# Two layers of attention over eight images: when the squares for the bound run, where the selected rows' products stand, how the weighted sums are grouped in image 1, and how many filler matmuls stand in the tail

## The chip, the cores and the metric

The kernel runs on one core of one Trainium2 chip. The metric is the device time in microseconds of one execution, and the number of a kernel is the median of its runs. The core has five engines that run side by side: TensorE (PE in the rows, with its weight loads as PEld), VectorE (DVE), ScalarE (ACT), GpSimd (POOL) and SyncE (SP, which here only issues DMAs). Each works through its own list of instructions in order and waits on semaphores for the others.

## What is computed

Eight images of 32 x 32 positions and 128 channels go through two blocks. The first is a normalisation, full attention with 8 heads of 16 channels over all 1024 positions, a projection and a residual. The second projects, normalises, and lets each position attend to 16 of 64 pooled keys, the 16 with the largest score over all heads and positions:

```python
# layer 0, for each image
qkv = layernorm(x) @ w_qkv + b_qkv
attn = softmax(q @ k.T * HEAD_DIM ** -0.5)          # 8 heads, 1024 x 1024
x = x + (attn @ v) @ w_out + b_out
# layer 1
tokens = x @ Win + b_in
t = layernorm(tokens); q, k, v = t @ Wq, t @ Wk, t @ Wv
pk, pv = pool4x4(k), pool4x4(v)                      # 64 pooled positions
red = (q @ pk.T).max(over heads and positions)       # 64 numbers
idx = top_k(red, 16)
tokens = tokens + softmax(q @ pk[idx].T * scaling) @ pv[idx]
tokens = tokens + gelu(layernorm(tokens) @ Wf1 + bf1) @ Wf2 + bf2
out = tokens @ Wout + bout
```

## The kernel before

**The steps.** Layer 0's attention of an image is cut into 32 steps (`STEPS`): four pairs of heads, each with eight blocks of 128 keys. In a step TensorE computes the scores of one key block for two heads and all queries in two halves c = 0 and 1 (`scores`, L616, into the two halves of the PSUM tile `S`), ScalarE takes the exponential of each half (L850, `Pr<-S`), and TensorE multiplies with the values (`weighted`, L631, into `O`). Each half of `S` has one buffer, so the scores of step s, half c, wait for the exponential of step s-1, half c (`probs_ready`). `Pr` holds three steps.

**Grouping of the weighted sums.** In images 0 and 7 the weighted sum of step s-1 follows the scores of step s. In the others two sums, of s-2 and s-1, follow the scores of each even step. After each eighth step VectorE turns the finished `O` of the head pair (`divide_o`, L1067 to L1074: transpose, reciprocal, product, transpose); the first weighted sum of the next pair waits for the first of these (`o_turned`).

**The work between.** Other work is hung on the steps by hand. `before_tasks(n + 1, s)` prepares the next image: transposes of xn, q and k (steps 17 to 23), v, the squares' sums for a bound (`AT_BOUND` = 28) and a flag (30); with steps above 32 it runs in the image itself (the `tokx` products at 32 and 37, steps 0 and 5 of the image). `after_tasks(n - 1, s)` does layer 1 of the image before, by a table of steps (`USUAL`, and `ENDING` for the last two images): `tok` at step 3, `t` 12, `q1` 13, `pk` 15, scores against pooled keys 18 to 21, `rt` 22 and `rb` 23. At `rb` VectorE ranks the 64 maxima (L1154 to L1163) and writes `hot`, the one-hot rows of the ranks (`hot_ready`). At `sel` TensorE multiplies `hot` with the pooled keys and values (L696, L698), VectorE writes `bd_k` and `bd_v` from it, and at `s2` (step 27) TensorE multiplies by `bd_k` (L645).

**GpSimd.** Within an image it moves `tokx`, computes `means_share` and `q1_rest`, normalises the image after the next, and then in `square(n)` (L488) squares `qh` and `kh` of the next image, once VectorE has drained k at step 23. The sums of these squares are a bound on the scores; TensorE uses them at step 28. Behind it stand the copies of the next image's values (`place_v`).

**The tail.** Image 7's layer 1 and the end of image 6's come after all attention (`tail()`). There TensorE has little work between waits, and ahead of certain steps it runs filler matmuls whose result is not used (L834, two for each count in `WARM`).

In the trace a matmul on f32 operands appears as two instructions, so a weighted sum of one step is 8 rows of L631 in it and 4 in the order of the program; the scores (f32r) appear as 4 in both.

Of the kernel before, what the change touches and what calls it, by code (L numbers as in the profile page):

```python
# [31 lines left out]
IMAGES, SIDE, C = 8, 32, 128  # L32
# [8 lines left out]
STEPS = PAIRS * TILES  # L41
# [13 lines left out]
AT_XN, AT_XN_SECOND = (6, 10), (8, 10)  # L55
AT_Q, AT_K, AT_V, AT_TOKX = (17, 19), (21, 23), (25, 29), (32, 37)
AT_BOUND, AT_FLAG = 28, 30
After = namedtuple("After", "tok norm1 t q1 pk sc rt rb sel s2 exp2 e2 pt tok2 norm2 tt2 t2 ff gelu wout out")
USUAL = After(tok=3, norm1=8, t=12, q1=13, pk=15, sc=(18, 19, 20, 21), rt=22, rb=23, sel=26, s2=27, exp2=28, e2=28, pt=30,
              tok2=31, norm2=34, tt2=33, t2=37, ff=(39, 39), gelu=39, wout=40, out=(41, 43))  # L60
ENDING = After(tok=3, norm1=8, t=12, q1=13, pk=14, sc=(17, 18, 19, 20), rt=21, rb=22, sel=23, s2=24, exp2=25, e2=25, pt=27,
               tok2=28, norm2=30, tt2=29, t2=32, ff=(33, 33), gelu=33, wout=34, out=(35, 36))
# [3 lines left out]
def tail():  # L66

    last = [(IMAGES - 1, s) for s in range(AFTER_END)]
    before = [(IMAGES - 2, s) for s in range(STEPS, AFTER_END)]
    k, m = ENDING.wout - STEPS, ENDING.tok + 1  # L70
    return before[:k] + last[:m] + before[k:] + last[m:]


def plan(n):

    return ENDING if n >= IMAGES - 2 else USUAL


def one_by_one(n):

    return n in (0, IMAGES - 1)


def xn_steps(n):
# [1 line left out]
    return AT_XN_SECOND if n == 1 else AT_XN  # L86


WARM = {ENDING.tok: 4, ENDING.t: 28, ENDING.pk: 8, ENDING.sc[0]: 36, ENDING.sel: 8, ENDING.pt: 16, ENDING.t2: 22, ENDING.out[0]: 8}
WAKE = 24  # L90

K_TOK, K_T, K_Q1, K_PK, K_PV, K_SC, K_RT, K_RB, K_SELK, K_SELV = 0, 2, 4, 6, 7, 8, 16, 17, 18, 19
# [38 lines left out]
def two_layers(nc, x, ln_scale, ln_bias, w_qkv, b_qkv, w_out, b_out, Win, b_in, Wq, Wk, Wv, g1, be1, g2, be2,  # L131
# [11 lines left out]
    with ExitStack() as ctx:  # L143
        def sb(name, shape, dt=fp32):
            return ctx.enter_context(nc.sbuf_tensor(name, shape, dt))

        def sem(name):
            return ctx.enter_context(nc.semaphore(name))
# [37 lines left out]
        tok, tT, q1T = sb("tok", [P, TILES, C]), sb("tT", [P, T]), sb("q1T", [P, T])  # L186
# [59 lines left out]
        pooled_ready, hot_ready = sem("pooled_ready"), sem("hot_ready")  # L246
# [12 lines left out]
        def a_after(n, use, i):  # L259

            return a_turn_of[n, use, i] + 1
# [14 lines left out]
        def wait_for_flag(eng, n):  # L276

            if n == 0:
                eng.wait_ge(first_dve, FIRST_FLAG)
            else:  # L280
                eng.wait_ge(a_drained, a_after(n, "flag", 0))
# [142 lines left out]
        def _(pool):  # L424
            def wait(signal, value):

                pool.wait_ge(signal, value)
                pool.sem_inc(pool_passed, 1)
# [55 lines left out]
            def square(n):  # L484

                wait(a_drained, a_after(n, "k", 1))
                for i, part in enumerate((qh, kh)):
                    ins = pool.tensor_tensor(squares[:, i, :], part[:, :].bitcast(fp32), part[:, :].bitcast(fp32), ALU.mult)  # L488
                ins.then_inc(squares_ready, 1)
# [12 lines left out]
            def image(n):  # L502

                if n > 0:
                    place_v(n, 3)
                    wait(b_drained[1], b_after(n - 1, K_TOK + 1))
                    wait(a_drained, a_after(n, "tokx", 1))
                else:
                    wait(first_dve, FIRST_DVE)
                pool.tensor_tensor(tokx[:, :, :], tokx_new[:, :, :], tok_bias[:, :].unsqueeze(1).to_broadcast([P, TILES, C]),  # L510
                                   ALU.add).then_inc(tokx_moved, 1)
                if n == 0:
                    normalise(1)
                if n + 1 < IMAGES:
                    means_share(n + 1)
                if n > 0:
                    q1_rest(n - 1)
                if n == 0:
                    square(1)
                if n + 2 < IMAGES:  # L520
                    normalise(n + 2)
                if 0 < n < IMAGES - 1:
                    square(n + 1)
                if n + 1 < IMAGES:
                    for j in range(3):
                        place_v(n + 1, j)
# [7 lines left out]
        def _(pe):  # L534
# [49 lines left out]
            def row_maxima(n):  # L584

                for j in range(PAIRS):
                    pe.wait_ge(stack_in[j], 32 + 16 * STACK_DMAS * (n + 1))
                if n > 0:
                    pe.wait_ge(probs_ready, 2 * STEPS * n)
                pe.sem_inc(pe_passed, 1)  # L590
                with pe.Fori(0, TILES) as t:
                    pe.wait_ge(tile_copied, TILES * n + t + 1)
                    for h in range(HEADS):
                        pe.wait_ge(max_drained, MAX_TILES * n + HEADS * t + h + 1)
                        r = 64 * (h % 2)
                        for c in range(2):
                            mm = pe.matmul(S[:, h % 2, c * HALF:(c + 1) * HALF], Qt[r:r + MROW, h // 2, :],
                                           Ks[r:r + MROW, h // 2, c * HALF:(c + 1) * HALF], start=True, stop=True)
                        mm.then_inc(max_filled, 1)
                pe.wait_ge(max_drained, 2 + MAX_TILES * (n + 1))  # L600
                pe.sem_inc(pe_passed, 1)
                pe.transpose(S[0:MAX_TILES, 0, 0:P], mx[:, :], ident[:, :]).then_inc(max_turned, 1)
                pe.wait_ge(mneg_ready, n + 1)
                pe.wait_ge(mrow_in, 16 * HEADS * (n + 1))

            def scores(n, s, c):

                j, kb = s // TILES, s % TILES
                before = 2 * STEPS * n + 2 * s + c - 1
                if before > 0:  # L610
                    pe.wait_ge(probs_ready, before)
                if kb == 0 and c == 0:
                    pe.wait_ge(stack_in[j], 32 + 16 * STACK_DMAS * (n + 1))
                for a in range(2):
                    head = slice(64 * a, 64 * a + MROW + 1)
                    mm = pe.matmul(S[:, c, a * HALF:(a + 1) * HALF], Ks[head, j, kb * P:(kb + 1) * P],  # L616
                                   Qs[head, j, c * HALF:(c + 1) * HALF], start=True, stop=True)
                mm.then_inc(scores_ready, 1)

            def weighted(n, s):  # L620

                j, kb = s // TILES, s % TILES
                pe.wait_ge(probs_ready, 2 * STEPS * n + 2 * s + 2)
                if kb == 0:
                    pe.wait_ge(va_ready, PAIRS * n + j + 1)
                    if n > 0 or j > 0:
                        pe.wait_ge(o_turned, PAIRS * n + j)
                for a in range(2):
                    for c in range(2):
                        r = 32 * (2 * a + c)  # L630
                        mm = pe.matmul(O[r:r + 32, :], Va[:, kb, 2 * j + a, :], Pr[:, (STEPS * n + s) % 3, c, a * HALF:(a + 1) * HALF],  # L631
                                       start=(kb == 0), stop=(kb == TILES - 1))
                mm.then_inc(pv_done, 1)
# [161 lines left out]
            def image(n):  # L795

                wait_for_flag(pe, n)
                pe.sem_inc(pe_passed, 1)
                with pe.If(pe.value_load(flag[0:1, 0:1], min_val=0, max_val=HEADS) > 0):
                    row_maxima(n)  # L800
                with pe.Else():
                    pe.sem_inc(max_filled, MAX_TILES)
                    pe.sem_inc(max_turned, 1)
                for s in range(STEPS):
                    scores(n, s, 0)
                    scores(n, s, 1)
                    if s > 0 and (s % 2 == 0 or one_by_one(n)):
                        if not one_by_one(n):
                            weighted(n, s - 2)
                        weighted(n, s - 1)  # L810
                    if n > 0:
                        before_tasks(n, STEPS + s)
                    if n + 1 < IMAGES:
                        before_tasks(n + 1, s)
                    if n > 1:
                        after_tasks(n - 2, STEPS + s)
                    if n > 0:
                        after_tasks(n - 1, s)
                if not one_by_one(n):
                    weighted(n, STEPS - 2)  # L820
                weighted(n, STEPS - 1)

            image(0)

# [4 lines left out]
            for n, s in tail():  # L829
                for _ in range(WARM.get(s, 0) if n == IMAGES - 1 else 0):  # L830

# [496 lines left out]
```

## Time and profile before

| | us |
|---|---|
| median of 3 runs | 860.02 |
| the 3 runs | 860.02, 855.59, 860.54 |
| profiled execution, its own time | 855.3 |
| its span, first to last instruction | 853.6 |
| PE, ACT, DVE, POOL busy in the span | 796.4, 603.8, 519.4, 163.7 |
| mean granted TensorE clock | 0.972 |

All times of rows are microseconds from the start of the span. A row of the timeline gives start, duration, engine, line, operation and tiles; in square brackets stands how long the engine was idle just before and what ended the wait. The granted clock is a share of full speed: 1.00 is 2.4 GHz, 0.50 is 1.2 GHz.

### The profile page before, as it was taken

To read this page: it belongs to the slowest core of one execution; us is meant where nothing else is said; L and a number is where in the kernel's file an instruction comes from. 1 tells how busy PE (TensorE), PEld (TensorE's weight loads), DVE (VectorE), ACT (ScalarE), POOL (GpSimd) and SP (SyncE) were. 2 spreads that over 40 slices of the span, in tenths; PEclk is the share of its full clock that TensorE was granted. 3 is DMA by queue.
4 is the path that set the end of the run, shared out by engine and by line. 5 is a ranking of instruction groups with operands and counts; after the bars stand their busy time and mean duration, and the time that the engine had idled before them with its cause. 6 is when DMAs were issued, how large, how long until landed. Compare 5 with 4: busy or idle time off the path is not lost.

```text
span 853.6 us, 14509 instructions
## 1 busy us (share of the span) xinstructions
PE 796.4 (93%) x5155; PEld 382.9 (45%) x5155; DVE 519.4 (61%) x1518; ACT 603.8 (71%) x683; POOL 163.7 (19%) x198
## 2 busy tenths in 40 slices
PE   8889888999999999999999999999999989899988
PEld 6322332345443545345434544344533534246675
DVE  6405434678567775678567765767467853467464
ACT  3697775777887788777886788768876787682112
POOL 1620520410341031220241033202111011000100
PEclk9999987999999999999999999999999999899979
DMA  3553341422442251432342352323152232201300
GB/s 67 96 90 65 64 81 31 100 47 49 82 98 46 48 87 45 104 63 48 66 109 45 52 97 66 75 48 63 26 122 47 43 66 50 56 7 31 76 1 25
DMA packets 45309, 52.91 MB, mean 62 GB/s; under 512 B 15920, under 2 KB 33968, under 8 KB 45232
## 3 DMA queue, kind: packets, MB, share of 16 engines
q1 hardware_dynamic: 45232, 51.92, 31.3%
q8 instruction: 43, 0.70, 0.3%
q14 instruction: 34, 0.28, 0.1%
HBM read 5.45 MB, written 4.19 MB: 11 GB/s over the span
## 4 chain that ended last, share of the span: by engine, by line
PE 61%; ACT 13%; DVE 8%; issue 5%; ACTq 0%; DVEq 0%
PE O L631 21%; PE S L616 13%; ACT Pr L850 9%; PE BC L645 6%; PE BC L637 3%; PE S L834 3%; PE BC L742 2%; PE BC L682 2%; PE BC L728 2%; PE A L569 2%; PE BC L664 2%; DVE rsel L1159 1%; DVE rgt L1158 1%; ACT hT L890 1%; ACT L850 1%
## 5 line engine op out<-in xcount | busy, mean ns | idle before, releaser
L850 ACT ACTIVATE Pr<-S 128x1024 f32<-128x1024 f32 x512 | 491.0, 1029 | 136.3 <-PE S L616 132.8
L631 PE MATMUL O<-Pr,Va 128*32 128x512 f32 x2048 | 263.7, 623 | 8.5 <-DVE OT L1067 7.8
L616 PE MATMUL S<-Qs,Ks 49*128 49x512 f32 x1024 | 217.5, 470 | 30.2 <-ACT Pr L850 27.4
L616 PEld LDWEIGHTS S<-Qs,Ks 49*128 49x128 f32 x1024 | 87.8, 185 | 173.2 <-ACT Pr L850 132.4
L631 PEld LDWEIGHTS O<-Pr,Va 128*32 128x32 f32 x2048 | 51.9, 111 | 117.1 <-issue 96.3
L496 POOL TENSOR_TENSOR q1l<-q1T,q1h 128x1024 fp32r<-128x1024 f32 x8 | 19.1, 2389 | 226.5 <-DVE q1h L1117 226.5
L1141 DVE TENSOR_REDUCE r<-BC 128x1 f32<-128x512 f32 x64 | 41.3, 684 | 29.8 <-PE BC L682 29.4
L1067 DVE STREAM_TRANSPOSE OT<-O 128x512 f32<-128x512 f32 x32 | 22.8, 713 | 55.1 <-PE O L631 54.9
L459 POOL TENSOR_SCALAR xn<-X,ln 128x128 f32<-128x128 f32 x56 | 45.8, 830 | 3.9 <-DVE ln L980 3.9
L865 ACT ACTIVATE tT<-BC,cols 128x512 f32<-128x512 f32 x32 | 23.4, 779 | 31.5 <-PE BC L637 31.4
L510 POOL TENSOR_TENSOR tokx<-tokx_new,tok_bias 128x1024 f32<-128x1024 f32 x8 | 18.9, 2366 | 121.0 <-DVE tokx_new L986 121.0
L488 POOL TENSOR_TENSOR squares<-qh 128x1024 bf16<-128x1024 f32 x7 | 13.6, 1937 | 140.5 <-DVE kl L994 140.5
L1208 DVE TENSOR_SCALAR hT<-BC,cols 128x512 f32<-128x512 f32 x32 | 24.0, 751 | 25.0 <-PE BC L728 23.5
L470 POOL COPY Va<-v_new 128x256 f32<-128x256 f32 x32 | 11.9, 399 | 139.8 <-PE O L631 120.8
L1213 DVE TENSOR_TENSOR Y<-BC,out_bias 128x512 f32<-128x512 f32 x16 | 11.0, 690 | 45.1 <-PE BC L742 45.1
L481 POOL TENSOR_SCALAR tokx_new<-win_sum,ln 128x128 f32<-128x128 f32 x64 | 37.4, 607 | 1.4 <-POOL tokx L510 1.3
L834 PE MATMUL S<-Qs,Ks 49*128 49x512 f32 x260 | 33.6, 410 | 0.0
L728 PE MATMUL BC<-tT,wf_s 128*128 128x512 f32 x64 | 31.7, 616 | 1.1 <-ACT tT L865 0.5
L682 PE MATMUL BC<-Q1s,K1s 96*128 96x512 f32 x64 | 29.7, 539 | 3.2 <-issue 2.2
L742 PE MATMUL BC<-w2o,hT 128*128 128x128 f32 x256 | 32.2, 280 | 0.0
L742 PEld LDWEIGHTS BC<-w2o,hT 128*128 128x128 f32 x256 | 29.6, 192 | 5.1 <-issue 5.1
L569 PE MATMUL A<-xnT,wqkv_s 128*128 128x512 f32 x56 | 31.5, 645 | 0.0
(189 smaller groups left out, 995.6 us busy)
## 6 DMA issues: line engine op xcount, KB each, us to landing
Qs<-qh SPq DMA_DIRECT2D x128, 64.0 KB, 2.3
Ks<-kh SPq DMA_DIRECT2D x128, 64.0 KB, 2.3
Q1s<-q1h SPq DMA_DIRECT2D x64, 128.0 KB, 2.4
X<-in_x_dram SPq DMA_DIRECT2D x8, 512.0 KB, 4.0
Qs<-ql SPq DMA_DIRECT2D x64, 64.0 KB, 2.4
Ks<-kl SPq DMA_DIRECT2D x64, 64.0 KB, 2.3
attnT<-On SPq DMA_DIRECT2D x128, 32.0 KB, 2.0
Q1s<-q1l SPq DMA_DIRECT2D x32, 128.0 KB, 2.4
```

Source lines behind the costliest of these rows:

```text
L459: ins = pool.tensor_scalar(xn[:, t, :], X[:, t, :], ln[:, 0, t:t + 1], ln[:, 1, t:t + 1], ALU.subtract, ALU.mult)
L481: ins = pool.tensor_scalar(tokx_new[:, t, :], win_sum[:, :], ln0[n % 2][:, 0, t:t + 1], None, ALU.mult)
L569: pe.matmul(A[:, :], wqkv_s[:, c:c + C], half(xnT, h), start=True, stop=True).then_inc(a_filled, 1)
L616: mm = pe.matmul(S[:, c, a * HALF:(a + 1) * HALF], Ks[head, j, kb * P:(kb + 1) * P], Qs[head, j, c * HALF:(c + 1) * HALF], start=True, sto ...
L631: mm = pe.matmul(O[r:r + 32, :], Va[:, kb, 2 * j + a, :], Pr[:, (STEPS * n + s) % 3, c, a * HALF:(a + 1) * HALF], start=(kb == 0), stop=(k ...
L645: mm = pe.matmul(bank[:, t * P:(t + 1) * P], lhs[:, c:c + P], w, start=(i == 0), stop=(i == len(pairs) - 1))
L682: pe.matmul(bank[:, :], K1s[:, j, :, :].rearrange("p a b -> p (a b)"), half(Q1s[0:ROWS1, j, :], h), start=True, stop=True).then_inc(filled, 1)
L728: pe.matmul(bank[:, :], wf1_s[:, f * C:(f + 1) * C], half(tT, h), start=True, stop=True)\
L742: mm = pe.matmul(BC[h][:, t * P:(t + 1) * P], hT[:, f, c:c + P], w2o[:, f, :], start=False, stop=(t == 3 and f == 1))
L834: pe.matmul(S[:, 0, a * HALF:(a + 1) * HALF], Ks[head, 0, 0:P], Qs[head, 0, 0:HALF], start=True, stop=True)
L850: act.activation(Pr[:, g % 3, c, :], S[:, c, :], ACT.Exp, scale=SCALE).then_inc(probs_ready, 1)
L1141: ins = dve.tensor_reduce(r8[:, 2 * j + h:2 * j + h + 1], bank[:, :], AX.X, ALU.max)
```

## The change

There are four edits. `square(n)` for n > 1 also waits for `hot_ready` of the image whose ranks are computed in the same stretch. `sel` in `USUAL` moves from step 26 to 25 (images 0 to 5, whose layer 1 runs inside images 1 to 6). In image 1 the weighted sums of steps 0 to 11 are issued one by one, each behind the scores of the next step; from step 14 on they go in pairs as before. And `WARM` is smaller at four places of the tail (`t` 28 to 8, `sel` 8 to 4, `pt` 16 to 12, `t2` 22 to 20) and has no entry any more for `out[0]` (8 before).

```diff
+LIGHT = 13
-USUAL = After(... rt=22, rb=23, sel=26, s2=27, exp2=28, ...
+USUAL = After(... rt=22, rb=23, sel=25, s2=27, exp2=28, ...
...
-def one_by_one(n):
-
-    return n in (0, IMAGES - 1)
+def sums_behind(n, s):
+
+    if n in (0, IMAGES - 1) or (n == 1 and s < LIGHT):
+        return (s - 1,) if s > 0 else ()
+    return (s - 2, s - 1) if s % 2 == 0 and s > 0 else ()
...
-WARM = {ENDING.tok: 4, ENDING.t: 28, ENDING.pk: 8, ENDING.sc[0]: 36, ENDING.sel: 8, ENDING.pt: 16, ENDING.t2: 22, ENDING.out[0]: 8}
+WARM = {ENDING.tok: 4, ENDING.t: 8, ENDING.pk: 8, ENDING.sc[0]: 36, ENDING.sel: 4, ENDING.pt: 12, ENDING.t2: 20}
...
             def square(n):
 
                 wait(a_drained, a_after(n, "k", 1))
+                if n > 1:
+                    wait(hot_ready, n - 1)
...
-                    if s > 0 and (s % 2 == 0 or one_by_one(n)):
-                        if not one_by_one(n):
-                            weighted(n, s - 2)
-                        weighted(n, s - 1)
+                    for behind in sums_behind(n, s):
+                        weighted(n, behind)
...
-                if not one_by_one(n):
-                    weighted(n, STEPS - 2)
-                weighted(n, STEPS - 1)
+                for behind in sums_behind(n, STEPS):
+                    weighted(n, behind)
```

How the change stands in the order of instructions, at three places. On TensorE at the start of image 1, from step 0 to the transposes of xn behind step 6 (`S` scores, `O` weighted sums, `A` the tokx products and the transposes of xn, `BC` the product for tok), before:

```order
143 L616 MATMUL S<-Qs,Ks 128x512 x4
144 L645 MATMUL A<-win_s,xhT 128x128 x4
145 L616 MATMUL S<-Qs,Ks 128x512 x8
146 L631 MATMUL O<-Pr,Va 32x512 x8
147 L616 MATMUL S<-Qs,Ks 128x512 x4
148 L645 MATMUL BC<-wow,attnT 128x128 x8
149 L616 MATMUL S<-Qs,Ks 128x512 x4
150 L631 MATMUL O<-Pr,Va 32x512 x8
```

and now, in the same stretch (each line number is higher by five on TensorE in the changed file):

```order
143 L621 MATMUL S<-Qs,Ks 128x512 x4
144 L650 MATMUL A<-win_s,xhT 128x128 x4
145 L621 MATMUL S<-Qs,Ks 128x512 x4
146 L636 MATMUL O<-Pr,Va 32x512 x4
147 L621 MATMUL S<-Qs,Ks 128x512 x4
148 L636 MATMUL O<-Pr,Va 32x512 x4
149 L621 MATMUL S<-Qs,Ks 128x512 x4
150 L636 MATMUL O<-Pr,Va 32x512 x4
151 L650 MATMUL BC<-wow,attnT 128x128 x8
```

The first weighted sum stood behind the scores of step 2 and now stands behind those of step 1, and so on at each odd step. On TensorE at steps 24 to 27 of image 1 (in images 2 to 6 the same rows stand there), before:

```order
193 L616 MATMUL S<-Qs,Ks 128x512 x4
194 L631 MATMUL O<-Pr,Va 32x512 x8
195 L616 MATMUL S<-Qs,Ks 128x512 x4
196 L645 MATMUL A<-wqkv_s,xnT 128x128 x4
197 L616 MATMUL S<-Qs,Ks 128x512 x4
198 L631 MATMUL O<-Pr,Va 32x512 x8
199 L696 MATMUL BC<-hot,pkv 128x16
200 L698 MATMUL BC<-pkv,hot 128x128
201 L616 MATMUL S<-Qs,Ks 128x512 x4
202 L645 MATMUL BC<-bd_k,q1T 128x128 x8
```

and now:

```order
203 L621 MATMUL S<-Qs,Ks 128x512 x4
204 L636 MATMUL O<-Pr,Va 32x512 x8
205 L621 MATMUL S<-Qs,Ks 128x512 x4
206 L650 MATMUL A<-wqkv_s,xnT 128x128 x4
207 L701 MATMUL BC<-hot,pkv 128x16
208 L703 MATMUL BC<-pkv,hot 128x128
209 L621 MATMUL S<-Qs,Ks 128x512 x4
210 L636 MATMUL O<-Pr,Va 32x512 x8
211 L621 MATMUL S<-Qs,Ks 128x512 x4
212 L650 MATMUL BC<-bd_k,q1T 128x128 x8
```

The two products with `hot` have moved ahead of the scores of step 26 and the weighted sums behind them. On GpSimd in image 1, before:

```order
37 L488 TENSOR_TENSOR squares<-qh 128x1024 [waits a_drained]
38 L488 TENSOR_TENSOR squares<-kh 128x1024
39 L470 COPY Va<-v_new 128x8x2x16 [waits a_drained,pv_done] x4
```

and now:

```order
37 L493 TENSOR_TENSOR squares<-qh 128x1024 [waits a_drained,hot_ready]
38 L493 TENSOR_TENSOR squares<-kh 128x1024
39 L473 COPY Va<-v_new 128x8x2x16 [waits a_drained,pv_done] x4
```

The order on GpSimd is the same; the first of the two squares has a second wait, and the copies of the values stand behind it.

## Rows read from the trace of the kernel before

**Rows 1.** The page's chain that ended last, by engine.

```profile
PE 61%; ACT 13%; DVE 8%; issue 5%; ACTq 0%; DVEq 0%
```

**Rows 2.** Waits of the whole span: total us, times, longest us.

```profile
PE O L631 <- DVE OT L1067: 7.8, 9, 1.2
```

**Rows 3.** Timeline, image 1, steps 23 and 24 and later: VectorE and GpSimd.

```profile
176.11 1.94 POOL L488 TENSOR_TENSOR squares<-qh 128x1024 bf16<-128x1024 f32 x1 [15.73 <-DVE kl L994]
...
176.58 1.52 DVE L1158 TENSOR_SCALAR rgt<-rB,rcol 64x64 f32<-64x64 f32 x1
...
178.03 1.96 DVE L1159 SCALAR_TENSOR_TENSOR rsel<-rB,rcol,below 64x64 f32<-64x64 f32 x1
...
180.52 0.28 DVE L1163 TENSOR_SCALAR hot<-iota_f,rank 64x128 f32<-64x128 f32 x1
180.72 0.70 DVE L1067 STREAM_TRANSPOSE OT<-O 128x512 f32<-128x512 f32 x1
...
194.32 1.08 POOL L470 COPY Va<-v_new 128x256 f32<-128x256 f32 x3 [14.42 <-PE O L631]
```

**Rows 4.** Timeline of TensorE, image 1: v (25), scores (26), sums (24, 25), s2 (27).

```profile
178.04 1.16 PE L645 MATMUL A<-wqkv_s,xnT 128*128 128x128 f32 x8
...
179.92 0.50 PE L616 MATMUL S<-Qs,Ks 49*128 49x512 f32 x2 [0.28 <-ACT Pr L850]
...
181.57 1.92 PE L631 MATMUL O<-Pr,Va 128*32 128x512 f32 x16 [1.15 <-DVE OT L1067]
...
184.53 2.05 PE L645 MATMUL BC<-bd_k,q1T 128*128 128x128 f32 x16
```

**Rows 5.** Three lines of VectorE over the whole span: duration ns min/median/max.

```profile
L1158 DVE TENSOR_SCALAR rgt<-rB,rcol x8: 246/1521/1523, 176.6 to 814.8; 64x64 f32<-64x64 f32 x8
...
L1159 DVE SCALAR_TENSOR_TENSOR rsel<-rB,rcol,below x8: 271/1958/1959, 178.0 to 814.9; 64x64 f32<-64x64 f32 x8
...
L1070 DVE TENSOR_TENSOR OT<-OT,rden x32: 424/424/1415, 47.9 to 771.0; 128x256 f32<-128x256 f32 x32
```

**Rows 6.** Timeline of ScalarE in image 0.

```profile
37.50 3.78 ACT L850 ACTIVATE Pr<-S 128x1024 f32<-128x1024 f32 x4 [0.18 <-PE S L616]
...
48.57 3.77 ACT L850 ACTIVATE Pr<-S 128x1024 f32<-128x1024 f32 x4
...
53.84 3.77 ACT L850 ACTIVATE Pr<-S 128x1024 f32<-128x1024 f32 x4
```

**Rows 7.** Timeline of TensorE, image 1: scores of step 0, scores of step 13.

```profile
104.19 0.73 PE L616 MATMUL S<-Qs,Ks 49*128 49x512 f32 x4 [0.67 <-issue]
...
146.58 0.73 PE L616 MATMUL S<-Qs,Ks 49*128 49x512 f32 x4
```

**Rows 8.** Busy us: PE, PEld, DVE, ACT, POOL; granted clock, DMA share, GB/s.

```profile
30.00:104.00 74.00, 66.22 (x417) 20.20 (x417) 25.33 (x84) 62.49 (x68) 24.77 (x31) 1.00 0.43 78
104.10:146.60 42.50, 35.73 (x198) 13.99 (x198) 17.84 (x79) 27.81 (x31) 7.05 (x10) 0.80 0.30 57
```

**Rows 9.** Timeline of the tail: fillers (L834) and what stands behind them.

```profile
784.04 6.64 PE L834 MATMUL S<-Qs,Ks 49*128 49x512 f32 x56
...
785.12 2.13 DVE L1083 TENSOR_SCALAR that<-tok,ln 128x128 f32<-128x128 f32 x8
...
813.92 3.78 PE L834 MATMUL S<-Qs,Ks 49*128 49x512 f32 x16
...
815.75 0.28 DVE L1163 TENSOR_SCALAR hot<-iota_f,rank 64x128 f32<-64x128 f32 x1
...
827.20 0.66 PE L637 MATMUL BC<-ident,E 128*128 128x128 f32 x4 [0.41 <-DVE E L1190]
...
837.58 0.66 PE L637 MATMUL BC<-ident,that 128*128 128x128 f32 x4 [0.37 <-DVE that L1083]
...
842.45 2.00 ACT L890 ACTIVATE hT<-hT 128x1024 f32<-128x1024 f32 x2
844.26 2.11 PE L834 MATMUL S<-Qs,Ks 49*128 49x512 f32 x16
```

More of the change, by code:

```diff
@@ L57 @@
 AT_BOUND, AT_FLAG = 28, 30
+LIGHT = 13
 After = namedtuple("After", "tok norm1 t q1 pk sc rt rb sel s2 exp2 e2 pt tok2 norm2 tt2 t2 ff gelu wout out")
-USUAL = After(tok=3, norm1=8, t=12, q1=13, pk=15, sc=(18, 19, 20, 21), rt=22, rb=23, sel=26, s2=27, exp2=28, e2=28, pt=30,
+USUAL = After(tok=3, norm1=8, t=12, q1=13, pk=15, sc=(18, 19, 20, 21), rt=22, rb=23, sel=25, s2=27, exp2=28, e2=28, pt=30,
               tok2=31, norm2=34, tt2=33, t2=37, ff=(39, 39), gelu=39, wout=40, out=(41, 43))
```

## The prediction

> **What bounds the kernel now.** I read the chain that ended last first: 61% of it is TensorE, 13% ScalarE, 8% VectorE [rows 1]. So a microsecond in which TensorE waits for VectorE or ScalarE is the thing to look for, and the table of waits gives one that repeats: the weighted sums wait for the transpose of O nine times, 7.8 us in all [rows 2]. The timeline shows where. In image 1, at step 24, VectorE computes the ranks while GpSimd squares qh: GpSimd starts at 176.11, and VectorE's comparison L1158 takes 1.52 us, the next, L1159, 1.96 us beside the squares of kh, so that hot is written from 180.52 and the transpose of O starts at 180.72 only [rows 3]. TensorE has waited 1.15 us for that transpose when it starts the sums of steps 24 and 25 at 181.57 [rows 4]. Both comparisons have a minimum of 246 and 271 ns, which is what they take in the tail, where no squares run; their medians are 1521 and 1958 [rows 5]. Six images (1 to 6) have this stretch, and six such waits are 6.9 of the 7.8 us.
>
> The second place is the start of image 1: 42.4 us from the scores of step 0 to those of step 13 [rows 7]. PE is busy in 35.7 of 42.5 us, ACT in 27.8, and the granted clock averages 0.80, so 40% of this stretch ran at 1.2 GHz, the rest at 2.4; image 0, with single sums, ran at 1.00 throughout with PE busy in 66.2 of 74.0 us [rows 8]. The third is the tail, where rows of fillers end later than what they cover [rows 9].
>
> **Squares behind hot, and sel at step 25.** The three cannot be costed apart. Without squares beside them L1158 and L1159 take 0.25 and 0.27 us [rows 5]. L1158 still starts at 176.58; from the end of L1159 (179.99) to the end of hot (180.80) it is 0.8 us [rows 3], so hot is done at 176.58 + 0.52 + 0.8 = 177.9 instead of 180.8. The transpose of O follows at once (0.70 us) and is done at 178.6, before TensorE wants it: its wait goes. The squares start at about 178.1 and run to 182.0, 2 us later than now. Behind them stand the copies of the values, which waited 14.42 us for TensorE and start at 194.3 [rows 3], and the squares' sums at step 28, which are more than 5 us off; so GpSimd's new wait costs nothing there. Without this cover it would be 2 us an image.
>
> What the squares now run beside is divide_o. Its product L1070 takes 424 ns, but once 1415 [rows 5]: that is image 0, step 24, where the squares ran beside it. So I take 1.0 us of delay: transpose to 178.6, reciprocal 178.9, product to 180.1, the second transpose 180.8, v 181.5, bd_k 181.8. If it is held up by both squares, bd_k comes at about 183.6.
>
> On the page "SBUF — State Buffer" of the Trainium skill, section "Who interferes with whom", stands a rule against this move: a VectorE instruction with two SBUF inputs and a GpSimd instruction that reads SBUF exclude each other, and the later one waits for the whole of the other. By that rule the move shifts the hold-up from two instructions to one, L1070, which would wait for up to the 1.9 us of one square; the row's 1415 ns agrees. Transposes and reciprocals have one SBUF input and would go free.
>
> TensorE then runs v from 178.04 to 179.1 [rows 4], the products with hot (two short pairs, 0.55 us: the time by which the scores of step 27 stand off the sums before them now) to 179.7, the scores of step 26 to 180.6 (their second half has to wait for ScalarE until 179.9 in any case [rows 4]), the sums 1.85 to 182.45, the scores of step 27 0.65 to 183.1, and then s2. It stood at 184.53 [rows 4]: 1.43 us gained. From there the pattern is the same and bound by PE and ACT, so the gain is kept; the DMAs do not move, since sel issues none and SP waits for other things. bd_k at 181.8 has 1.3 us to spare. Range for one image: 0.9 if L1070 waits for both squares, 1.7 if the products with hot vanish in waits for ScalarE. Sum: 6 x 1.45 = **8.7 us** (5.4 to 10.2).
>
> **Single sums in image 1.** Image 0 is the model. Two steps without a task take 3.78 + 0.18 = 3.96 us there, and two with the transposes of xn 53.84 - 48.57 = 5.27, so 1.31 more [rows 6]. Thirteen steps are 25.7 us. On them come two tokx products of 1.1 (eight 128 x 128 instructions, as v in [rows 4]), tok with 2.0 (sixteen, as s2 there), xn twice 1.3, t 1.0, and 0.3 for the transpose of O, for which single sums do wait at step 9 though pairs don't: 33.8 us. It was 42.4 [rows 7]: **8.6 us**. Most of that is the clock. In a pair TensorE waits for ScalarE without a sum to fill the wait, then does two sums at once while ScalarE runs dry; at 1.2 GHz such a pair of sums is longer than both exponentials. The bounds: if the clock stays at 0.80, I keep only what the waits give, some 3 us; the upper end, 9.5, is the tasks in part hidden behind ScalarE, whose own work there is 27.8 us [rows 8]. I take the value of image 0, since the same instructions in the same order stand there.
>
> **Fewer fillers.** At t there are 16 instead of 56. They start at 784.04, take 6.64 us for 56 and so 1.9 for 16, until 786.0; the first half of `that`, written from 785.12 in 2.13 us, is ready at 786.2 and the second at 787.3 [rows 9]. The transposes start at 786.3 instead of 790.6. The second half follows one microsecond later and not at once, but ScalarE took them one after the other anyway: 4.3 us. At sel, 8 instead of 16: the 16 ran from 813.92 for 3.78 us at the lower clock, hot was done at 816.03 [rows 9]. With 8 TensorE waits for hot: 1.1 to 1.5 us, or nothing where the clock is high, as 16 then end at 816.0 too; I take 1.0. At pt and t2 the second half of the input ends the wait (0.41 and 0.37 us behind VectorE [rows 9]), so taking 8 and 4 away gives nothing. At out, 16 instructions of 2.11 us from 844.26 go; the gelu, started at 842.45 with 2.00 us for both halves, has its first half ready at 843.5 and its second at 844.5, before TensorE asks for it [rows 9]: 2.0 us. Sum **7.3 us** (4.3 to 7.9).
>
> **The sum.** 8.7 + 8.6 + 7.3 = 24.6 us. Against the profiled execution's own 855.3 (span 853.6 and 1.7 around it) that is 830.7. The median of the runs is 860.02, 4.7 above it, and the runs lie in two groups, at 855.6 and 860. If that is stretches at the lower clock in image 1 or in the tail, it goes with them; if it is elsewhere it stays. I add a part of it: **832 us**.
>
> **Rivals.** (1) *The clock in image 1 stays as it was.* For: it fell there though TensorE was busy for most of the stretch, and image 1 has more tasks than image 0. Against: image 0, with single sums, never fell [rows 8]. Gain there 3 instead of 8.6: 838. (2) *The clock falls in the tail where fillers went.* For: the fillers exist, and at 813.92 they ran at the lower clock even so [rows 9]. 16 of them take 3.78 us at the lower and 2.11 at the upper level, so necessary TensorE work costs 0.8 us more per microsecond; some 8 us of it between 786 and 797 or behind 838 give 6 us back: 838. The Trainium skill, page "TensorE: Matmul & The Clock Gate", section "Why this matters for your kernels", says that idle gaps between bursts of matmuls bring the lower clock. By it the new gaps ahead of the transposes would decide; no row here shows a gap alone doing so. (3) *The hold-up only moves.* L1070 waits for both squares, the v drain and bd_k come late, s2 waits: 0.5 an image or less instead of 1.45, 838. For: VectorE's L1159 waited out the whole of the second square. Against: L1158 got in between the two, and L1070 in image 0 too. (4) *Slower.* Both thin stretches run at the lower clock from end to end, since TensorE there is never dense enough again: image 1's start has about 28 us of TensorE work at full speed (13 x 1.66, scores 0.7 and sums 0.96 by [rows 4], and the tasks), times 1.8 is 50, 8 us more than now; the tail adds 15 to its time and loses its gain. With 8.7 gained in the images that is about +14, 870. It decides only once over 30 us of TensorE's own work more than now runs at the lower clock.
>
> **Chances.** Forecast 0.6 (828 to 836 by its own terms). Rivals 1, 2 and 3 one by one 0.14, 0.12 and 0.07, all faster; two of them at once with the 4.7 us of the median kept, 844 to 852, 0.05; slower 0.02. The range from 826 to 842 leaves out under 2 in 10. About 1% is what a measurement of this kernel can tell from no change, that is 851.4 and 868.6: faster 0.95, the same 0.03, slower 0.02.
>
> **What the new profile would show.** Right: L1158 and L1159 near 250 and 270 ns in all images, L1070 at 1.4 us in six more images, no wait of the sums for OT at step 26, s2 about 5.1 us behind the start of v instead of 6.5; the scores of step 13 of image 1 some 34 us behind those of step 0, and the granted clock there above 0.95; the transposes of the tail's t behind `that` and not behind fillers; the last products right behind wout. Wrong: a TensorE wait for bd_k or hot, or a granted clock below 0.9 in either stretch.

## The result, and the profile after

| | before | after |
|---|---|---|
| median, us | 859.0 (4 runs, 855.59 to 860.54) | 826.28 (4 runs, 825.08 to 829.83) |
| profiled execution, us | 855.3 | 827.2 |
| span, us | 853.6 | 825.5 |
| mean granted clock | 0.972 | 0.983 |

The ratio is 0.9631, with a 95% interval of 0.9587 to 0.9675: 32.7 us by the medians, 28.1 by the profiled executions. (The fourth run of before was taken with the changed kernel.) The ratios here and below leave out two of the ten runs of pairs_fill, which fell in a slower state, and each differs a little, by up to 0.25%, from the ratio of the two medians.

The two spans can be cut at three instructions that both have: the scores of step 0 of image 1, the scores of its step 13, and the last weighted sums of image 7. The table tells where the 28.1 us of the profiled executions are.

| stretch | before | after | gained | forecast |
|---|---|---|---|---|
| start to step 0 of image 1 | 104.2 | 102.5 | 1.7 | 0 |
| image 1, step 0 to step 13 | 42.4 | 32.2 | 10.2 | 8.6 |
| from there to the last weighted sums | 622.2 | 612.7 | 9.5 | 8.7 |
| tail | 84.8 | 78.1 | 6.7 | 7.3 |

The first row is no work of the change: the first scores start at 27.33 instead of 29.04. In the trace of before, TensorE's first products (L763) fell in a stretch at the lower clock, in that of the changed kernel they did not. The windows 13.4 to 16.8 us, before and then after (busy us of PE, PEld, DVE, ACT, POOL; granted clock, DMA share, GB/s):

```profile
13.40:16.80 3.40, 3.40 (x4) 1.31 (x5) 0.61 (x1) 1.65 (x3) 0.00 (x0) 0.50 0.00 0
```
```profile
13.40:16.80 3.40, 3.40 (x8) 1.41 (x9) 1.18 (x2) 2.70 (x5) 0.00 (x0) 1.00 0.00 0
```

In the thirteen traces of these kernels the first scores start at 26.9 to 27.7 where the clock was full until then, and at 28.1 to 30.8 where it was not.

**The ranks.** One row of each line over the whole span (duration ns min/median/max), the answer to [rows 5], for the changed kernel:

```profile
L1160 DVE TENSOR_SCALAR rgt<-rB,rcol x8: 246/247/248, 164.9 to 790.1; 64x64 f32<-64x64 f32 x8
...
L1161 DVE SCALAR_TENSOR_TENSOR rsel<-rB,rcol,below x8: 270/271/272, 165.1 to 790.3; 64x64 f32<-64x64 f32 x8
...
L1072 DVE TENSOR_TENSOR OT<-OT,rden x32: 424/425/1416, 46.2 to 749.6; 128x256 f32<-128x256 f32 x32
```

The maxima of the two comparisons are now within 2 ns of what their minima were. The hold-up has moved to the product in divide_o: it takes 1.41 to 1.42 us once in each of images 0 to 6, where before it did so in image 0 alone. The timeline of image 1 at the same place as [rows 3, 4], after:

```profile
165.87 0.28 DVE L1165 TENSOR_SCALAR hot<-iota_f,rank 64x128 f32<-64x128 f32 x1
166.07 0.70 DVE L1069 STREAM_TRANSPOSE OT<-O 128x512 f32<-128x512 f32 x1
...
166.33 1.89 POOL L493 TENSOR_TENSOR squares<-qh 128x1024 bf16<-128x1024 f32 x1 [17.63 <-DVE hot L1165]
166.35 1.16 PE L650 MATMUL A<-wqkv_s,xnT 128*128 128x128 f32 x8
...
167.09 1.41 DVE L1072 TENSOR_TENSOR OT<-OT,rden 128x256 f32<-128x256 f32 x1
167.44 0.39 PE L701 MATMUL BC<-hot,pkv 64*128 64x16 f32 x2
...
168.66 1.93 PE L636 MATMUL O<-Pr,Va 128*32 128x512 f32 x16
...
169.75 0.28 DVE L1170 TENSOR_TENSOR bd_k<-BC,head_mask 128x128 f32<-128x128 f32 x1
...
171.17 2.05 PE L650 MATMUL BC<-bd_k,q1T 128*128 128x128 f32 x16
```

The transpose follows hot at once, the weighted sums start without a wait, bd_k is ready 1.1 us before s2 wants it, and s2 starts 4.82 us behind v; before it was 6.49 [rows 4].

**Image 1.** The answer to the second row of [rows 8] (busy us of PE, PEld, DVE, ACT, POOL; granted clock, DMA share, GB/s), after:

```profile
104.10:138.00 33.90, 30.81 (x198) 12.07 (x197) 17.86 (x80) 29.50 (x35) 7.13 (x9) 1.00 0.38 71
```

The clock is full throughout. TensorE at the start of the image, after:

```profile
102.48 0.73 PE L621 MATMUL S<-Qs,Ks 49*128 49x512 f32 x4 [0.70 <-issue]
...
106.49 0.91 PE L621 MATMUL S<-Qs,Ks 49*128 49x512 f32 x4
...
134.66 0.73 PE L621 MATMUL S<-Qs,Ks 49*128 49x512 f32 x4
```

Steps 0 and 1 with the tokx products between them take 4.01 us, which is 3.96 for two steps and next to nothing for the products.

**The tail.** Fillers and what stands behind them, after, the answer to [rows 9]:

```profile
762.60 2.12 PE L836 MATMUL S<-Qs,Ks 49*128 49x512 f32 x16
763.69 2.13 DVE L1085 TENSOR_SCALAR that<-tok,ln 128x128 f32<-128x128 f32 x8
764.85 0.66 PE L642 MATMUL BC<-ident,that 128*128 128x128 f32 x4
...
789.27 2.07 PE L836 MATMUL S<-Qs,Ks 49*128 49x512 f32 x8
...
791.10 0.28 DVE L1165 TENSOR_SCALAR hot<-iota_f,rank 64x128 f32<-64x128 f32 x1
...
791.43 0.61 PE L701 MATMUL BC<-hot,pkv 64*128 64x16 f32 x2
```

The transposes now wait for `that`, and the products with hot for hot. The distance from the last sums (768.79 before, 747.38 after) to the transposes fell from 21.8 to 17.5 us, from hot's start to s2 (818.52 before, 792.62 after) from 2.8 to 1.5, and from s2 to the end by 2.2. Between the transposes and hot 1.1 us came back. The lower clock covered the last 8.5 us of that distance now and the last 7.0 before, which may account for part of it.

**What does not answer to any edit.** In image 7 TensorE waits at step 17 for the stack of Q1s (1.77 us before, 1.79 after), and in both traces the clock is lower from about that wait on. The profile names no releaser; in the program this step waits for the transfers of Q1s, the last of which SyncE issued from 700.23 on. The changed kernel, TensorE's row and the stretch behind it:

```profile
704.62 1.19 PE L687 MATMUL BC<-Q1s,K1s 96*128 96x512 f32 x2 [1.79 <-issue]
```
```profile
704.00:717.70 13.70, 13.08 (x44) 4.12 (x44) 3.87 (x6) 5.81 (x6) 0.00 (x0) 0.50 0.17 49
```

In the trace of before the lower clock lasted 6.8 us there, now 13.7. That is why the third stretch of the table gained only 9.5 us in this pair of traces, though the six stalls gave 13.2 (by the distances counted under p_square). The wait does not always bring the lower clock: in the trace of p_warm it is 1.78 us as well, and the clock stays full in image 7.

```profile
731.60 0.70 PE L682 MATMUL BC<-Q1s,K1s 96*128 96x512 f32 x2 [1.78 <-issue]
```
```profile
729.00:746.00 17.00, 14.61 (x95) 4.98 (x89) 8.67 (x21) 12.72 (x14) 0.00 (x0) 1.00 0.25 63
```

### The profile page after: what moved, and what is told of

Read it like the earlier page. It is cut to its first block, busy times and chain, and to the rows that moved or that the text cites. A ratio compares the mean times of both kernels' runs of the same rounds, so it can differ in the third digit from the quotient of the medians.

```text
span 825.5 us, 14363 instructions
## 1 busy us (share of the span) xinstructions
PE 778.4 (94%) x5079; PEld 373.3 (45%) x5079; DVE 506.5 (61%) x1518; ACT 604.1 (73%) x683; POOL 164.5 (20%) x198
## 4 chain that ended last, share of the span: by engine, by line
PE 62%; ACT 15%; issue 6%; DVE 5%; ACTq 0%; DVEq 0%
PE O L636 21%; PE S L621 15%; ACT Pr L852 10%; PE BC L650 6%; PE BC L642 3%; PE BC L687 3%; PE BC L733 2%; PE BC L747 2%; PE BC L669 2%; PE A L650 2%; PE A L574 2%; PE S L836 1%; ACT hT L892 1%; ACT L852 1%; ACT L892 1%
## 5 line engine op out<-in xcount | busy, mean ns | idle before, releaser
L636 PE MATMUL O<-Pr,Va 128*32 128x512 f32 x2048 | 256.7, 606 | 1.8 <-DVE OT L1069 1.1
L621 PE MATMUL S<-Qs,Ks 49*128 49x512 f32 x1024 | 217.3, 471 | 24.6 <-ACT Pr L852 22.0
L636 PEld LDWEIGHTS O<-Pr,Va 128*32 128x32 f32 x2048 | 50.0, 109 | 104.6 <-issue 96.9
L1143 DVE TENSOR_REDUCE r<-BC 128x1 f32<-128x512 f32 x64 | 41.4, 685 | 32.7 <-PE BC L687 32.5
L473 POOL COPY Va<-v_new 128x256 f32<-128x256 f32 x32 | 11.8, 399 | 112.9 <-PE O L636 95.5
L733 PE MATMUL BC<-tT,wf_s 128*128 128x512 f32 x64 | 31.7, 616 | 1.1 <-ACT tT L867 0.5
L886 ACT ACTIVATE E<-E 128x512 f32<-128x512 f32 x16 | 9.4, 632 | 26.8 <-DVE E L1182 26.7
```

Source lines behind the costliest of these rows:

```text
L733: pe.matmul(bank[:, :], wf1_s[:, f * C:(f + 1) * C], half(tT, h), start=True, stop=True)\
L1143: ins = dve.tensor_reduce(r8[:, 2 * j + h:2 * j + h + 1], bank[:, :], AX.X, ALU.max)
```

## The experiments

A set is a group of kernels measured together with the kernel before. All ratios are to the kernel before of the same set, whose median was 856 to 859 us; 859 us times one minus the ratio gives the gain. The intervals are 2 to 4.5 us to either side of a gain.

| kernel | median, us | ratio | interval |
|---|---|---|---|
| p_square | 844.77 | 0.9858 | 0.9826 to 0.989 |
| p_sel | 858.75 | 1.0022 | 0.9994 to 1.0051 |
| p_square_sel | 841.73 | 0.982 | 0.9781 to 0.9859 |
| p_single | 846.69 | 0.9876 | 0.985 to 0.9901 |
| p_warm | 849.36 | 0.9915 | 0.9889 to 0.9941 |
| pairs_fill | 851.08 | 0.9921 | 0.9882 to 0.9961 |
| squares_later | 825.19 | 0.9643 | 0.96 to 0.9686 |
| after_again | 826.61 | 0.961 | 0.9567 to 0.9652 |
| late_scores | 823.0 | 0.9615 | 0.9572 to 0.9657 |
| best | 821.57 | 0.957 | 0.9535 to 0.9604 |
| all_single | 881.69 | 1.0285 | 1.0234 to 1.0336 |

**The squares' wait alone (p_square)**, on the kernel before:

```diff
                 wait(a_drained, a_after(n, "k", 1))
+                if n > 1:
+                    wait(hot_ready, n - 1)
```

> Only the wait of the squares for hot is added to the kernel before; sel stays at step 26. Port theory (VectorE's two comparisons are held up by GpSimd's squares): the comparisons fall to 0.25 and 0.27 us in images 1 to 6, the sums of steps 24 and 25 no longer wait 1.15 us for OT, and s2 starts about 5.4 us behind v instead of 6.5: 6 to 7 us faster, and up to 3 more where the lower clock set in right behind the stall (images 5 and 6 of the trace of before). Rival (the stall only moves to divide_o's product, whose 424 ns become 1.4 us): below 2 us faster.

Measured: 12 us faster (0.9858). TensorE's rows in image 1, v, the second scores of step 26, the sums, s2:

```profile
178.24 1.16 PE L647 MATMUL A<-wqkv_s,xnT 128*128 128x128 f32 x8
...
180.11 0.50 PE L618 MATMUL S<-Qs,Ks 49*128 49x512 f32 x2 [0.28 <-ACT Pr L852]
180.54 1.92 PE L633 MATMUL O<-Pr,Va 128*32 128x512 f32 x16
...
183.50 2.05 PE L647 MATMUL BC<-bd_k,q1T 128*128 128x128 f32 x16
```

The sums start right behind the scores, and s2 stands 5.26 us behind v instead of 6.49: 1.23 an image, 7.4 in six. The stall theory holds and the rival falls. But 12 is more than 7.4. Most of the rest is in images 5 and 6 of the trace of before; the weighted sums of image 5 there, and the clock beside them:

```profile
556.22 3.56 PE L631 MATMUL O<-Pr,Va 128*32 128x512 f32 x16 [1.15 <-DVE OT L1067]
```
```profile
556.00:560.00 4.00, 3.78 (x20) 0.98 (x21) 2.04 (x5) 0.34 (x1) 0.00 (x0) 0.57 0.07 16
```

The same two sums take 3.56 us instead of 1.92 [rows 4], at the lower clock. From the rank's first product (rsel<-rB,ident on VectorE) to the first maximum behind s2 it is 9.6 us in four images of before and 11.3 in two. This distance, and the clock in it, in all traces:

| kernel | images 1 to 6, us | images with the lower clock there |
|---|---|---|
| before | 9.6 or 11.3 | 2 of 6 |
| p_sel | 9.6 or 11.2 | 4 of 6 |
| p_single | 9.6 or 11.3 | 4 of 6 |
| p_warm | 9.6 or 11.3 | 3 of 6 |
| pairs_fill | 9.6 or 11.2 to 11.3 | 2 of 6 |
| p_square | 8.4 | 0 of 6 |
| p_square_sel, after, after_again, squares_later, late_scores, best | 8.0 | 0 of 36 |
| all_single | 10.2, 11.8 or 14.2 | 3 of 6 |

In the five kernels with the stall the lower clock follows it in 15 of 30 images, at 1.65 us each; without the stall in none of 42. In all_single the sums wait again for the transpose of O, 1.04 us, though the comparisons are fast, and the lower clock is back in three of six images, as in image 2:

```profile
273.92 1.37 PE L634 MATMUL O<-Pr,Va 128*32 128x512 f32 x8 [1.04 <-DVE OT L1067]
```

So in the kernel before a stall costs 1.23 + 0.5 x 1.65 = 2.05 us on the mean, 12.3 us in six, which agrees with the 12 measured (9.4 to 14.9). The half is a share over five kernels, one trace of each; in the trace of before it was 2 of 6.

**sel alone (p_sel)**: `rb=23, sel=26` becomes `rb=23, sel=25`, with the squares as before.

> Only sel moves to step 25; the squares still start beside the ranks. If hot at 180.8 is the limit, TensorE stops at step 25 for hot instead of at step 26 for OT, so that ScalarE starves earlier: 0 to 3 us slower. Rival (the move by itself hides the products with hot in waits for ScalarE): 2 to 3 us faster.

Measured: 1.0022, an interval that holds 1. TensorE in image 1, at v and the products with hot:

```profile
180.34 1.16 PE L645 MATMUL A<-wqkv_s,xnT 128*128 128x128 f32 x8
...
183.15 0.39 PE L696 MATMUL BC<-hot,pkv 64*128 64x16 f32 x2 [1.65 <-DVE hot L1163]
```

TensorE stops for hot, 1.65 us, where it stopped for OT before; the end of the pattern does not move (9.59 against 9.64 us). The rival, 2 to 3 us faster, lies outside the interval and falls.

**Both (p_square_sel).**

> The kernel before with the squares behind hot and sel at step 25. Theory: with hot early, sel at 25 is worth 0.44 us an image, by the distance from the ranks to the maxima behind s2 (8.4 us with the squares' wait alone, 8.0 in the changed kernel): 14 to 15 us faster than before, 2 to 3 more than the wait alone; the lower clock in none of the six images behind the ranks. Rival (sel is worth nothing here either): 12 us.

Measured: 0.982, that is 15.5 us (12.1 to 18.8). The distance is 8.0 us in all six images, and sel is worth the 0.44 us an image between 8.4 and 8.0, 2.6 us. The intervals of this run and of p_square overlap, so the difference of medians alone would not show it; the traces do. The move of sel is worth something only once hot is early.

**Single sums alone (p_single)**: `sums_behind` with 13 for `LIGHT`, on the kernel before.

> Only the single sums in image 1. The stretch from the scores of step 0 to those of step 13 takes 32 to 33 us instead of 42.4, at a granted clock of 1.00 instead of 0.80: about 10 us faster. Rival (the clock there belongs to the phase of the run and not to the order): clock stays near 0.8 and 3 to 5 us faster.

Measured: 10.6 us faster, and the stretch takes 32.2 us (103.76 to 135.93) at full clock:

```profile
103.70:136.00 32.30, 29.18 (x198) 12.07 (x198) 16.59 (x71) 27.27 (x31) 7.13 (x9) 1.00 0.40 75
```

**Pairs with fillers (pairs_fill)**, on the kernel before, to part the clock from the waits:

```diff
+IDLE = {2: 3, 8: 6, 10: 4, 12: 6}
...
                 for s in range(STEPS):
+                    if n == 1 and s in IDLE:
+                        if s > 3:
+                            b_ready(0, K_TOK)
+                        for _ in range(IDLE[s]):
+                            pe.matmul(BC[0][:, 0:P], ident[:, :], ident[:, :], start=True, stop=True)
                     scores(n, s, 0)
```

> The kernel before (sums in pairs) with filler matmuls of the identity, whose result nobody reads, in front of the scores of steps 2, 8, 10 and 12 of image 1 (3, 6, 4 and 6 of them, about 0.25 us each), where TensorE waits for ScalarE. If the clock is what the single sums give back, the granted clock of the stretch from step 0 to step 13 rises to about 1.00 and it takes 36 to 37 us instead of 42.4, 5 to 6 us faster. Rival (the waits of the pairs are the loss and the clock follows from something else): 42 us or more, no gain.

Measured: the clock is full, and the scores of step 13 come 34.8 us behind those of step 0 (101.96 to 136.72).

```profile
101.90:136.80 34.90, 32.95 (x236) 16.96 (x236) 17.92 (x79) 27.38 (x31) 7.05 (x9) 1.00 0.37 69
```

So of the 10.2 us of image 1, 7.6 are the clock and 2.6 the waits that single sums fill. The gain of the whole, 0.9921 or 6.8 us (3.4 to 10.1), agrees with the 7.6. The matmuls here give nothing but activity, and in this trace they remove the loss: that the gaps brought the clock down is shown, and the rival falls. The ten runs of this kernel spread from 843 to 857 us and the traced one, 846, is among the fastest; where the clock was lower in the others is not known.

**Fillers alone (p_warm)**: the new `WARM` on the kernel before.

> Only the smaller fillers. Tail from the last weighted sums to the end 78 us instead of 84.8: 6 to 7 us faster, of which 4.3 at t, 2 at out and 0 to 1 at sel. Rival (TensorE's clock falls where the fillers went): below 3 us, with a granted clock under 0.9 between the t transposes and the products with wk.

Measured: 7.3 us faster (5.1 to 9.5). The tail is 76.9 us (768.58 to 845.5). The clock stayed full in this trace until 805.7, 20 us behind the fillers that were taken at t. The rival falls.

**The squares behind divide_o (squares_later)**, on the changed kernel:

```diff
-                if n > 1:
-                    wait(hot_ready, n - 1)
+                wait(on_ready, PAIRS * (n - 1) + 3)
```

> The changed kernel, but the squares wait until divide_o has written On of the third head pair, so that no VectorE instruction with two SBUF inputs runs beside them at step 24. Theory: the product L1072 falls from 1.4 to 0.42 us and the time does not move (within 1 us), since bd_k has over 1 us to spare. Rival (the stall has moved there and costs): 4 to 6 us faster.

Measured: 825.19 us and 0.9643, the same as the change. The product no longer waits anywhere:

```profile
L1071 DVE TENSOR_TENSOR OT<-OT,rden x32: 424/425/426, 47.9 to 749.1; 128x256 f32<-128x256 f32 x32
```

So the microsecond that the change moved to L1072 was free, as far as intervals of some 4 us either way can tell; in the trace s2 stands 4.8 us behind v as in the changed kernel.

**Scores a step later (late_scores)**, on the changed kernel:

```diff
-ENDING = After(... sc=(17, 18, 19, 20), rt=21, rb=22, sel=23, s2=24, exp2=25, e2=25, pt=27,
+ENDING = After(... sc=(18, 19, 20, 21), rt=22, rb=23, sel=24, s2=25, exp2=26, e2=26, pt=27,
```

> The changed kernel, with the scores against pooled keys and what follows one step later in images 6 and 7 (ENDING: sc 18 to 21, rt 22, rb 23, sel 24, s2 25, exp2 and e2 26). In image 7 TensorE waited 1.8 us for Q1s at step 17, and the lower clock followed for 13.7 us. If that wait brings the clock down, both go: 4 to 8 us faster. Rival (what the move saves there it loses where the ranks now come a step later): no change.

Measured: 823.0 us, about 3 less than the change where 4 to 8 were expected. TensorE finds Q1s there, and the distance from the ranks computed in image 6 to those computed in image 7 is 91.7 us instead of 97.5, though the latter stand a step later. TensorE's row:

```profile
705.43 0.73 PE L687 MATMUL BC<-Q1s,K1s 96*128 96x512 f32 x2
```

The lower clock is gone behind this place, but 3.4 us of it stand later in image 7, from 731.2 on. The ratio's interval overlaps that of the change, so the next set has both side by side.

**The change again, and both additions (after_again, best).**

> The changed kernel as it is, as the measure for the two others of this set: 825 to 828 us, the lower clock in image 7 behind the wait for Q1s in its trace.

> The changed kernel with the scores against pooled keys a step later in images 6 and 7, and with the squares behind divide_o. Theory (the wait for Q1s in image 7 and the lower clock behind it cost 4 to 6 us, the place of the squares nothing): 821 to 823 us, 3 to 5 faster than the changed kernel of this set. Rival: no difference.

Measured in one set: 826.61 (821.46 to 829.12) and 821.57 (819.89 to 823.27), 5 us by the medians, 3.7 by the means. The intervals of the two ratios still overlap: four of the six runs of the change are slower than every run of best, and the other two, 821.46 and 821.71, had a granted clock of 0.990 as best has. That fits a wait that the lower clock follows in some executions only; in the trace of after_again it lasted 6.8 us there. The clock in best where the changed kernel had 0.50:

```profile
690.00:717.70 27.70, 26.98 (x171) 9.78 (x169) 13.46 (x28) 24.15 (x27) 2.39 (x1) 1.00 0.34 82
```

Best has the lowest median here, 4.3% below the kernel before.

**Single sums everywhere (all_single)**, on the changed kernel: `sums_behind` returns `(s - 1,)` for all n and s > 0.

> The changed kernel with single sums in all steps of all images. If singles are better wherever ScalarE waits for scores, ScalarE's waits (120 us in all) shrink and it is 5 us or more faster. Rival (in images 2 to 6 TensorE is the bound, pairs or not, and a single sum stops TensorE where a pair finds its probabilities ready): no change or up to 5 us slower.

Measured: 881.69 us, 55 more than the change; the rival's sign, and ten times its size. The waits of ScalarE for scores (total us, times, longest), first the changed kernel, then this one:

```profile
ACT Pr L852 <- PE S L621: 119.8, 119, 6.3
```
```profile
ACT Pr L850 <- PE S L619: 179.3, 121, 7.3
```

The waits grew by 60 us. In the trace the other tasks hang on odd and even steps unevenly: a step with a task of 2 to 4 us now also has its own sums, so that ScalarE runs dry, and a step without a task waits for ScalarE with nothing to do. Pairs shift the sums to the even steps. That is read from the timeline, not tried by itself. Part of the loss is the lower clock: 0.967 over the span, against 0.983 in the changed kernel. As an estimate, the missing share of the clock times the span is 29 us here and 14 there, so some 15 of the 55 us.

## Why the prediction was right, and where its sizes were off

**The bound.** That TensorE's waits in six stretches, image 1's start and the tail were the places holds: the parts measured alone make 15.5 (squares and sel), 10.6 (single sums) and 7.3 (fillers), 33.4 us together, and the whole is 31.7 by the ratio of the first set and 33.5 by that of after_again. They add up within their intervals, so no large part of one gain rests on another. The three terms of the sum, 24.6 us, were too small by 7 to 9. The forecast also counted 3.4 of the 4.7 us between the profiled execution and the median as gained, and even so the time, 826.28 for 832, lies only 0.3 us inside the low end of the range, 826; squares_later, which does the same work, came out at 825.19. That the time fell inside is in part luck.

**Squares and sel: right mechanism, size 8.7 for 15.5.** The working of one image was right: the distance from v to s2 shrank by 1.67 for a forecast 1.43 (10 us in six images, still inside the term's 5.4 to 10.2), L1072 took 1.41 us for 1.4, and GpSimd's later copies cost nothing. What the step "1.45 an image" lacked is the clock: it was read from image 1, where the sums behind the stall ran at full clock, and so the 12.1 to 18.8 us measured lie above the term's own range. Images 5 and 6 of the same trace had 1.65 us more at this place, and the profiled execution of before was a fast one: at 855.3 it is below all four timed runs. The 4.7 us between it and the median may belong here in part, which the sum left open; no trace of an execution near the median is there to show it.

**The rule on the shared port** was borne out. The trace agrees with "Who interferes with whom" of the page "SBUF — State Buffer" of the Trainium skill in both directions: the two comparisons at 246 and 271 ns when nothing of GpSimd's runs and at 1521 and 1958 beside its squares [rows 5], and the two-input product at 1416 beside them, while transposes and reciprocals beside the squares keep their 0.71 and 0.26 us. The product waited for one square and not for both, and squares_later shows no price at the new place.

**Single sums: 8.6 for 10.2.** Image 0 as a model gave 33.8 us; it was 32.2. What was too large is the first tokx product, charged 1.1 and hidden at the start of the image, and another 0.5 us from step 6 on, among the transposes of xn, t and the wait for OT. "Most of that is the clock" is shown by pairs_fill: 7.6 of 10.2.

**Fillers: 7.3 for 6.7 in the trace, 7.3 in p_warm.** At t 4.35 for 4.3, at sel 1.25 for 1.0, at out and behind 2.2 for 2.0, pt and t2 nothing; 1.1 us came back where the clock was lower between.

**The rivals.** (1) and (2), a clock that stays or falls, did not come: the clock was 1.00 in the first 13 steps of image 1 in all seven kernels with single sums there, and full behind t. (3), that the hold-up only moves, did not come either: s2 stands 4.82 us behind v, and squares_later shows the moved one to be free. (4), slower, is far off.

**What stays open.** Why the lower clock follows a stall in one image and not in the next of the same run; only how often and at what price was measured. The same holds for the wait for Q1s in image 7, where it lasted from nothing (p_warm) to 13.7 us. And why all_single loses as much as it does: no run parts its share of clock from that of waits.

## What to carry to other kernels

A wait of TensorE can cost more than its length, here 2.05 us on the mean for 1.23, when the lower clock follows it: price it with the distances in all repetitions of the pattern and not with one, and compare the profiled execution with the median. Before moving a task earlier, look at who produces its input: sel was worth nothing until GpSimd's squares, an engine far from the critical path, no longer stood in VectorE's way. Single or paired issue is a matter of what hangs on each step: single sums won 10 us where steps were thin, and lost over 50 when they stood in all images, probably because the tasks hang on the steps unevenly.

## What the runs showed of the hardware that was not expected

A stall of 1.15 us (1.65 in p_sel) was followed by TensorE at 1.2 GHz in 15 of 30 images, the two sums behind it taking 3.56 instead of 1.92 us; none of 42 images without the stall showed it, and with another wait of 1.04 us at the same place (all_single) it was back in 3 of 6. The page "TensorE: Matmul & The Clock Gate" of the Trainium skill, section "Why this matters for your kernels", warns of gaps between bursts of matmuls; here single waits of 1.0 to 1.7 us between matmuls were followed by the lower clock in half of the images. At the start of image 1, fillers in the waits of the pairs (pairs_fill) raised the granted clock from 0.80 to 1.00. In the tail the lower clock set in behind the first scores against pooled keys, 1.6 to 5.5 us after they started in all thirteen traces, though 72 fillers stood right before them.
